# Three exponentials ahead of each pair of silus, a held GpSimd product, and a new set of places, in a fused Mamba and SwiGLU layer

## The chip, the cores and the metric

The kernel runs on one core of a Trainium2 chip. A core has five engines that run their own instruction lists and meet only at semaphores: TensorE (PE, matrix products and transposes into PSUM), VectorE (DVE), ScalarE (ACT, functions by table), GpSimd (POOL, which works on SBUF alone) and SyncE (SP, which issues transfers). The metric is the time of one launch on the device, in microseconds.

## The reference, cut to what matters

One layer over 4 sequences of 2048 rows of 256 values (8192 rows), all in float32:

```python
x_and_res = x @ W_in                                  # 256 -> 512 + 512
x_in, res = split(x_and_res)
x_conv = silu(causal_depthwise_conv4(x_in))           # "u" below
dt, B, C = split(x_conv @ W_x)                        # 16, 16, 16 columns
delta = softplus(dt @ W_dt + b_dt)
h = exp(delta * A) * h + delta * B * x_conv           # per row, 16 states for each of 512 channels
y = sum over states of C * h, plus x_conv * D
x = layernorm(x + (y * silu(res)) @ W_out)
gate, up = x @ wg.T, x @ wu.T                         # 256 -> 768, integer weights / 127
x = layernorm(x + (silu(gate) * up) @ wd.T)
```

The recurrence over the rows is the part that can't be made a matrix product. The 512 channels are 4 blocks of 128 partitions, so there are 64 recurrences (16 states by 4 blocks) for each stretch of rows.

## The kernel before, in words

The rows are cut into 16 chunks of 512 columns (time runs along the free axis). A chunk has 64 **beats**; beat b is state b // 4 and channel block b % 4. In each beat

- ACT computes `da = exp(delta * a)` (`exp`, L1086), into one of two PSUM banks in turn;
- POOL computes the product `dbu = du * B` (`times_b`, L1228) into one of DBU = 4 buffers of SBUF; the product of beat b waits until the scan of beat b - 4 has ended;
- DVE runs the scan `h = da * h + dbu` (`scan`, L1423);
- PE transposes h in 128 x 128 blocks (`turns`, L729), so that the sum over the 16 states can be taken with C as a per-partition scalar: half of the rows by ACT (`weigh`, L1095) and PE's accumulation (L754), the other half by DVE (`sum_states`, L1435, after each odd beat, 30 times in a chunk).

Everything else is fitted around the beats, with half a beat as the unit. While chunk i is scanned, the front of chunk i + 1 (the projection `xin` and `res`, the convolution `conv`, `dtb`, `ct`, `dt`) and the back of chunk i - 1 (turning the sums `yt`, the output projection `o`, the layer norm, turning its result `x1t`, `gate`, `up`, `down`, the second layer norm) are worked off. Their order is a table written by a planner: FILL_AT says in which beat PE issues each matmul group ("fill"), BANK in which of two PSUM banks it lands, READ_AT in which half beat ACT or DVE reads it, BEAT when the other steps of ACT and POOL come. A place of 64 and more means a beat of the next chunk, a negative one a beat of the chunk before. Nothing is dynamic: each engine's list has a fixed order, and an engine that waits holds up everything behind it. EARLY_FILL and EARLY_READ are the places of chunk 1's `xin` and `conv`, which are made during chunk 0. POOL has, beside its product in each beat, a tiny copy of the last column of h (`carry`, L1286) in each fourth beat, twelve more full-size products in a chunk (`times z` 4, L1279; `add u` 4, L1260; `times u` 4, L1267) and eight normalisations of 128 x 256 (L1252).

ACT holds one set of functions at a time. Exponential and logarithm are in one set, silu in another. So the silus of a chunk are gathered in two places ("windows"), each with a pair of them: `silu uz` (u of the next chunk and z, at 31 and 32) and `silu gate` (the two halves of the gates, at 43 and 45). At the start of a window ACT computes the exponentials of the next AHEAD = 2 beats at once, into buffers of SBUF called `da_ahead` (`between`, L1142), then loads the silu set (L1159), does the first silu, what lies between, the second one, loads the exponential set again (L1171), and computes the exponential of the beat after. The scans of these two beats (32 and 33, 44 and 45) read `da_ahead`, all other scans read a PSUM bank. Both kinds have the same line, L1423. The buffers are told apart in the trace by their names.

The normalisations of POOL lie at 27 (four, first layer norm) and at 96, 103, 108, 108 (second one, that is in beats 32, 39, 44, 44 of the chunk after). `times z` lies at 12, 12, 15, 17; `add u` at 52, 55, 62, 62 and `times u` at 53, 59, 63, 63.

## Time and profile before

| | |
|---|---|
| median of 3 runs | 1836.55 us (1835.42 to 1837.67) |
| profiled execution, its own time | 1836.67 us |
| its span | 1834.9 us |
| what lies around the span | 1.8 us |
| busy: DVE, PE, POOL, ACT | 1718.8, 1691.5, 1654.9, 1605.0 us |
| granted clock of TensorE, mean | 0.993 |

Busy is the time in which an engine had an instruction under way, waits for semaphores left out. All four are between 87% and 94% of the span, so no one of these shares names a bound. A scan, a product and an exponential are 128 x 512 float32 each. In the rows below the first number of a timeline line is the start in us from the span's start, the second the length; lines of the same kind that follow each other without a pause are put together, with their number behind the x; in brackets stands the idle time ahead of it and what ended that.

### The profile page before, as it was taken

To read this page: it belongs to the slowest core of one execution; us is meant where nothing else is said; L and a number is where in the kernel's file an instruction comes from. 1 tells how busy PE (TensorE), PEld (TensorE's weight loads), DVE (VectorE), ACT (ScalarE), POOL (GpSimd) and SP (SyncE) were. 2 spreads that over 40 slices of the span, in tenths; PEclk is the share of its full clock that TensorE was granted. 3 is DMA by queue.
4 is the path that set the end of the run, shared out by engine and by line. 5 is a ranking of instruction groups with operands and counts; after the bars stand their busy time and mean duration, and the time that the engine had idled before them with its cause. 6 is when DMAs were issued, how large, how long until landed. Compare 5 with 4: busy or idle time off the path is not lost.

```text
span 1834.9 us, 32556 instructions
## 1 busy us (share of the span) xinstructions
PE 1691.5 (92%) x10128; PEld 1270.3 (69%) x10128; DVE 1718.8 (94%) x1958; ACT 1605.0 (87%) x2769; POOL 1654.9 (90%) x1629
## 2 busy tenths in 40 slices
PE   8878898998989999898998989999898999988788
PEld 3546676776767677676776767677676776767667
DVE  4899999999999999999999999999999999999994
ACT  4797989989898998989889898998989899898874
POOL 2899899998999989999998999989899998999970
PEclk9999999999999999999999999999999999999999
DMA  7212213232222322313222322323222222211110
GB/s 239 104 59 104 82 59 121 73 119 71 104 92 70 115 71 104 105 66 119 78 108 72 113 82 73 113 70 115 94 82 104 82 104 81 105 70 58 35 47 24
DMA packets 82108, 164.57 MB, mean 90 GB/s; under 512 B 10369, under 2 KB 28033, under 8 KB 81938
## 3 DMA queue, kind: packets, MB, share of 16 engines
q1 hardware_dynamic: 80498, 160.90, 25.2%
q8 instruction: 85, 1.39, 0.3%
q10 hardware_dynamic: 1440, 1.58, 0.3%
q14 instruction: 85, 0.70, 0.1%
HBM read 87.47 MB, written 8.91 MB: 53 GB/s over the span
## 4 chain that ended last, share of the span: by engine, by line
PE 60%; ACT 16%; POOL 8%; issue 8%; DVE 6%; DMA 1%; DVEq 0%; SPq 0%; ACTq 0%; POOLq 0%
PE ht_upper L729 8%; PE ht_lower L729 8%; PE fill L665 8%; PE y_upper L754 8%; PE fill L551 7%; POOL dbu L1228 6%; PE fill L634 6%; DVE h L1423 5%; PE fill L655 3%; ACT da L1086 3%; PE fill L604 3%; PE fill L566 3%; ACT gt L1095 2%; ACT z L980 2%; PE fill L626 1%
## 5 line engine op out<-in xcount | busy, mean ns | idle before, releaser
L1228 POOL TENSOR_TENSOR dbu<-du,brep 128x512 f32<-128x512 f32 x1024 | 1315.2, 1315 | 115.0 <-DVE h L1423 88.5
L1423 DVE TENSOR_TENSOR_SCAN h<-da,carry,dbu 128x512 f32<-128x512 f32 x960 | 1184.5, 1268 | 41.7 <-ACT da L1086 37.1
L1086 ACT ACTIVATE da<-delta,a_s 128x512 f32<-128x512 f32 x960 | 654.8, 692 | 79.2 <-DVE h L1423 72.3
L1095 ACT ACTIVATE gt<-ht_upper,ct 128x512 f32<-128x512 f32 x512 | 350.1, 684 | 69.3 <-PE ht_upper L729 66.0
L729 PE MATMUL ht_upper<-ident,h 128*128 128x128 f32 x2048 | 314.8, 276 | 71.6 <-ACT gt L1095 51.0
L729 PEld LDWEIGHTS ht_upper<-ident,h 128*128 128x128 f32 x2048 | 242.6, 142 | 195.3 <-issue 130.7
L1435 DVE SCALAR_TENSOR_TENSOR acc<-ht_lower,ct,acc 128x512 f32<-128x512 f32 x480 | 349.2, 727 | 8.2 <-PE ht_lower L729 6.8
L729 PE MATMUL ht_lower<-ident,h 128*128 128x128 f32 x2048 | 312.3, 275 | 27.0 <-DVE acc L1435 23.0
L754 PE MATMUL y_upper<-ident,gt 128*128 128x128 f32 x2048 | 309.6, 274 | 0.9 <-ACT kb L912 0.9
L729 PEld LDWEIGHTS ht_lower<-ident,h 128*128 128x128 f32 x2048 | 239.2, 142 | 80.8 <-DVE h L1423 39.4
L754 PEld LDWEIGHTS y_upper<-ident,gt 128*128 128x128 f32 x2048 | 246.2, 141 | 51.1 <-issue 37.4
L551 PE MATMUL fill<-xt_s,win_s 128*128 128x512 f32 x456 | 223.3, 597 | 11.7 <-DVE x1t L1356 11.7
L665 PE MATMUL fill<-wd_s,kb 128*128 128x256 f32 x720 | 177.7, 380 | 0.0
L665 PEld LDWEIGHTS fill<-wd_s,kb 128*128 128x128 f32 x720 | 127.4, 190 | 18.3 <-issue 6.7
L634 PE MATMUL fill<-wout_s,kb 128*128 128x256 f32 x480 | 122.4, 383 | 0.7 <-DVE xr L1334 0.7
L1423 DVE TENSOR_TENSOR_SCAN h<-da_ahead,carry,dbu 128x512 f32<-128x512 f32 x64 | 118.6, 1874 | 0.0
L551 PEld LDWEIGHTS fill<-xt_s,win_s 128*128 128x128 f32 x456 | 74.5, 190 | 55.1 <-issue 55.1
L655 PE MATMUL fill<-x1t,wu_s 128*128 128x512 f32 x360 | 109.1, 431 | 0.4 <-DVE kb L1345 0.4
L655 PE MATMUL fill<-x1t,wg_s 128*128 128x512 f32 x360 | 106.5, 417 | 0.0
L634 PEld LDWEIGHTS fill<-wout_s,kb 128*128 128x128 f32 x480 | 85.3, 190 | 21.3 <-issue 12.8
L655 PEld LDWEIGHTS fill<-x1t,wu_s 128*128 128x128 f32 x360 | 64.2, 189 | 23.3 <-issue 6.7
L1260 POOL TENSOR_TENSOR delta<-delta,du 128x512 f32<-128x512 f32 x60 | 76.3, 1288 | 0.8 <-issue 0.3
(189 smaller groups left out, 1883.0 us busy)
## 6 DMA issues: line engine op xcount, KB each, us to landing
brep<-b_rows SPq DMA_DIRECT2D x127, 512.0 KB, 3.7
xs<-xin SPq DMA_DIRECT2D x242, 256.0 KB, 2.5
xr<-x SPq DMA_DIRECT2D x16, 512.0 KB, 5.5
xt_s<-x_t SPq DMA_DIRECT2D x15, 512.0 KB, 3.7
...
```

Of the source, the lines that this page charges most:

```text
L551: mm = nc.tensor.matmul(front_bank(c, name)[:, :], win_s[:, k, m * P:(m + 1) * P], xt_place(c)[:, k, :], start=(k == 0), stop=(k == KK - 1))
L634: mm = nc.tensor.matmul(fill_bank(name)[:, 0:DM], kb[:, m, t * P:(t + 1) * P], wout_s[:, m, :], start=(m == 0), stop=(m == DB - 1))
L655: mm = nc.tensor.matmul(fill_bank(name)[:, :], w[:, k, n * P:(n + 1) * P], x1t[:, half, k, :], start=(k == 0 and half == 0), stop=(k == KK ...
L665: mm = nc.tensor.matmul(fill_bank(name)[:, 0:DM], kb[:, n, t * P:(t + 1) * P], wd_s[:, n, :], start=(n == 0), stop=(n == HB - 1))
L729: mm = nc.tensor.transpose(bank[:, m * P:(m + 1) * P], h[:, n % 2, m, t * P:(t + 1) * P], ident[:, :])
L754: mm = nc.tensor.matmul(y_upper[m // 2][:, (m % 2) * HALF + k * P:(m % 2) * HALF + (k + 1) * P], lhsT=gt[:, (n * UPPER + k) % GT, m * P:(m ...
L1086: nc.scalar.activation(dst[:, :], delta[:, par, m, :], ACT.Exp, scale=a_s[:, m, n:n + 1])\
L1095: nc.scalar.activation(gt[:, (n * UPPER + k) % GT, :], ht_upper[:, :], ACT.Copy, scale=ct[:, par, k, n:n + 1])\
L1228: nc.gpsimd.tensor_tensor(dbu[:, beat % DBU, :], du[:, par, m, :], brep[:, n // PIECE % 2, n % PIECE, :], ALU.mult).then_inc(dbu_ready, 1)
L1260: nc.gpsimd.tensor_tensor(delta[:, par, m, :], delta[:, par, m, :], du[:, par, m, :], ALU.add)\
L1423: nc.vector.tensor_tensor_scan(h[:, n % 2, m, 0:T], da[beat % 2][:, :] if slot is None else da_ahead[:, slot, :], dbu[:, beat % DBU, :], c ...
L1435: nc.vector.scalar_tensor_tensor(out=acc[:, par, k, :], in0=ht_lower[:, :], scalar=ct[:, par, UPPER + k, n:n + 1], in1=acc[:, par, k, :], ...
```

## The change

- AHEAD is 3: the three exponentials of beats 31, 32, 33 and of beats 43, 44, 45 are made ahead, and three scans in each window read SBUF. `da_ahead` grows by a buffer. To make room, four small constants are put into one tensor.
- HOLD = (4, 5): the product of beat 35 (start of the first window, 30, + 1 + 4) waits until the scan of beat 33 has ended instead of that of beat 31, and the product of beat 48 (42 + 1 + 5) until that of beat 45 instead of 44.
- The windows move: `silu uz` to 30.5 and 32, `silu gate` to 42 and 43.5.
- All places are new: most fills, reads and norms lie half a beat to four beats earlier. `times z` lies at 7, 9, 13, 15, `add u` at 51, 55, 60, 63, `times u` at 52, 56, 63, 63, the first normalisations at 25, the second ones at 94, 100, 104, 112 (beats 30, 36, 40, 48).
- The early places of chunk 1's `xin` and `conv` are spread over beats 1 to 26 of chunk 0 instead of 0 to 16. Because of the new order, PE's first fill in each bank now waits for what chunk 0's front left there (`wait_first`).

```diff
-FILL_AT = {"xin1": (0, 1), "xin2": (1, 2), "xin3": (5, 5), "yt0": (7,), "yt1": (9,), "conv0": (9,),
...
+FILL_AT = {"xin2": (1, 1), "xin3": (3, 5), "yt0": (6,), "yt1": (7,), "conv0": (8,), "o0": (9, 9, 9, 10),
+           "o1": (11, 11, 11, 11), "conv1": (12,), "o2": (13, 14, 15, 15), "o3": (15, 16, 16, 16), "conv2": (18,),
+           "res0": (19, 21), "res1": (22, 24), "conv3": (22,), "x1t0": (24,), "x1t1": (25,), "res2": (29, 30),
+           "gate0": (31, 31), "res3": (32, 33), "gate1": (35, 35), "gate2": (37, 37), "gate3": (37, 37),
+           "gate4": (38, 38), "gate5": (38, 39), "dtb": (40, 40, 40, 41), "up0": (43, 43), "up1": (43, 43),
+           "up2": (44, 44), "ct": (45,), "dt0": (45,), "up3": (47, 47), "up4": (47, 48), "dt1": (48,), "dt2": (50,),
+           "up5": (50, 50), "down0": (51, 51, 51, 51, 53, 53), "dt3": (51,), "down1": (53, 55, 56, 56, 56, 56),
+           "xin0": (-10, -9), "down2": (56, 59, 59, 59, 59, 59), "down3": (60, 60, 60, 62, 63, 63), "xin1": (-1, -1)}
...
-EARLY_FILL = {"xin0": (0, 0), "xin1": (1, 1), "xin2": (2, 2), "xin3": (3, 3), "conv0": (5,), "conv1": (8,),
-              "conv2": (11,), "conv3": (14,)}
-EARLY_READ = {"xin0": 1, "xin1": 2, "xin2": 3, "xin3": 4, "conv0": 7, "conv1": 10, "conv2": 13, "conv3": 16}
+EARLY_FILL = {"xin0": (1, 1), "xin1": (3, 3), "xin2": (3, 4), "xin3": (6, 7), "conv0": (4,), "conv1": (12,),
+              "conv2": (18,), "conv3": (26,)}
+EARLY_READ = {"xin0": 1, "xin1": 5, "xin2": 5.5, "xin3": 8.5, "conv0": 9.5, "conv1": 13.5, "conv2": 22.5, "conv3": 26}
...
-BEAT = {"soft exp": [49, 51, 57, 59.5], "soft ln": [49, 52.5, 59.5, 59.5], "add u": [52, 55, 62, 62],
-        "times u": [53, 59, 63, 63], "x1 cut": [30, 35], "x1 low": [29.5, 30.5], "y upper": [5.5, 6],
-        "times z": [12, 12, 15, 17], "mean": [20.5, 73.5], "rstd": [25.5, 83], "shift": [27, 83],
-        "square": [(21, 21, 21, 23), (79.5, 79.5, 82, 82)], "norm": [(27, 27, 27, 27), (96, 103, 108, 108)],
-        "halo": -17.5, "silu uz": [31, 32], "silu gate": [43, 45]}
+BEAT = {"soft exp": [47.5, 51, 55, 57.5], "soft ln": [48.5, 52, 56, 59], "add u": [51, 55, 60, 63],
+        "times u": [52, 56, 63, 63], "x1 cut": [27, 29.5], "x1 low": [28, 28], "y upper": [5.5, 6.5],
+        "times z": [7, 9, 13, 15], "mean": [19, 67], "rstd": [23, 82], "shift": [25, 90],
+        "square": [(19.5, 19.5, 19.5, 20.5), (67, 75, 75, 76.5)], "norm": [(25, 25, 25, 25), (94, 100, 104, 112)],
+        "halo": -25.5, "silu uz": [30.5, 32], "silu gate": [42, 43.5]}
...
-AHEAD = 2
+AHEAD = 3
+DBU = 4
+HOLD = (4, 5)
...
+HELD = {start + 1 + HOLD[n]: start + AHEAD for n, start in enumerate(SILUS) if HOLD[n]}
+assert all(last < product < 64 and product - last <= DBU for product, last in HELD.items())
...
-        ones_row = sb("ones_row", [XD, 1])
-        convb_s = sb("convb_s", [P, DB])
-        d_s = sb("d_s", [P, DB])
-        eps_s = sb("eps_s", [P, 1])
+        consts = sb("consts", [P, 2 * DB + 2])
+        convb_s, d_s = consts[:, 0:DB], consts[:, DB:2 * DB]
+        ones_row, eps_s = consts[:, 2 * DB:2 * DB + 1], consts[:, 2 * DB + 1:2 * DB + 2]
...
+                elif (c, name) in held_before:
+                    wait_first([n for n in FIRST_FILLS if front_bank(0, n) is front_bank(c, name)][-1])
...
-                after(pool, h_ready, i * NH + beat + 1 - DBU)
+                used = beat - DBU if beat >= DBU else max(b for b in range(NH) if b % DBU == beat) - NH
+                after(pool, h_ready, i * NH + max(used, HELD.get(beat, used)) + 1)
```

READ_AT and BANK are new in the same way; of READ_AT the places that matter below are up0 and up1 at 44 (before 44.5 and 45), res2 at 32 (31.5), dtb at 43 (45).

## Rows read from the trace of the kernel before

**Rows 1.** Windows (length; busy: PE, PEld, DVE, ACT, POOL; PEclk, DMA): chunks 0, 1-14, 15, 4.
```profile
33.75:149.96 116.21, 88.23 (x479) 56.30 (x479) 101.36 (x98) 91.91 (x146) 102.83 (x97) 0.94 0.26 93
149.96:1685.43 1535.47, 1451.16 (x8784) 1096.96 (x8783) 1483.06 (x1653) 1395.84 (x2409) 1451.57 (x1424) 1.00 0.26 91
1685.43:1791.29 105.86, 85.07 (x535) 70.20 (x533) 103.81 (x114) 83.66 (x139) 93.52 (x93) 0.95 0.12 41
...
478.05:587.50 109.45, 103.80 (x631) 78.47 (x630) 106.13 (x121) 99.83 (x173) 103.83 (x103) 1.00 0.27 93
```

**Rows 2.** Groups by line: busy us, mean ns, idle before them, releasers.
```profile
L1228 POOL TENSOR_TENSOR dbu<-du,brep 128x512 f32<-128x512 f32 x1024 | 1315.2, 1315 | 115.0 <-DVE h L1423 88.5 <-DVE brep L1504 19.7 <-DVE du L1498 3.1
L1423 DVE TENSOR_TENSOR_SCAN h<-da,carry,dbu 128x512 f32<-128x512 f32 x960 | 1184.5, 1268 | 41.7 <-ACT da L1086 37.1 <-issue 2.6 <-POOL dbu L1228 1.8
...
L1423 DVE TENSOR_TENSOR_SCAN h<-da_ahead,carry,dbu 128x512 f32<-128x512 f32 x64 | 118.6, 1874 | 0.0
```

**Rows 3.** POOL's waits in chunk 4: total us, times, longest.
```profile
POOL dbu L1228 <- DVE h L1423: 4.7, 7, 1.8
POOL stats L1247 <- ACT stats L1006: 0.5, 1, 0.5
```

**Rows 4.** Timeline of DVE, first window of chunk 3 (beats 31 to 35).
```profile
418.81 0.72 DVE L1435 SCALAR_TENSOR_TENSOR acc<-ht_lower,ct,acc 128x512 f32<-128x512 f32 x1
419.45 4.08 DVE L1423 TENSOR_TENSOR_SCAN h<-da_ahead,carry,dbu 128x512 f32<-128x512 f32 x2
...
424.90 2.47 DVE L1423 TENSOR_TENSOR_SCAN h<-da,carry,dbu 128x512 f32<-128x512 f32 x2 [0.72 <-ACT da L1086]
```

**Rows 5.** Timeline of POOL, same window (products of beats 33 to 39).
```profile
417.52 3.76 POOL L1228 TENSOR_TENSOR dbu<-du,brep 128x512 f32<-128x512 f32 x3
421.19 1.15 POOL L1286 COPY carry<-h 128x4 f32<-128x4 f32 x1
422.44 3.39 POOL L1228 TENSOR_TENSOR dbu<-du,brep 128x512 f32<-128x512 f32 x2
426.26 2.53 POOL L1228 TENSOR_TENSOR dbu<-du,brep 128x512 f32<-128x512 f32 x2 [0.43 <-DVE h L1423]
428.73 0.19 POOL L1286 COPY carry<-h 128x4 f32<-128x4 f32 x1
```

**Rows 6.** Timeline of DVE, chunk 3's second window (from beat 44).
```profile
440.33 1.27 DVE L1423 TENSOR_TENSOR_SCAN h<-da_ahead,carry,dbu 128x512 f32<-128x512 f32 x1
442.24 0.69 DVE L1345 SCALAR_TENSOR_TENSOR kb<-fill,kb 128x512 f32<-128x512 f32 x1 [0.64 <-PE fill L655]
442.85 2.28 DVE L1423 TENSOR_TENSOR_SCAN h<-da_ahead,carry,dbu 128x512 f32<-128x512 f32 x1
```

**Rows 7.** Timeline of POOL, same window (products 45 to 47, 49 to 51).
```profile
437.98 4.69 POOL L1228 TENSOR_TENSOR dbu<-du,brep 128x512 f32<-128x512 f32 x3
...
445.21 1.27 POOL L1228 TENSOR_TENSOR dbu<-du,brep 128x512 f32<-128x512 f32 x1 [1.16 <-DVE h L1423]
448.24 2.54 POOL L1228 TENSOR_TENSOR dbu<-du,brep 128x512 f32<-128x512 f32 x2 [1.76 <-DVE h L1423]
```

**Rows 8.** Timeline, start of chunk 3: POOL's first products, DVE's first scans.
```profile
367.13 5.02 POOL L1228 TENSOR_TENSOR dbu<-du,brep 128x512 f32<-128x512 f32 x4
368.63 2.46 DVE L1423 TENSOR_TENSOR_SCAN h<-da,carry,dbu 128x512 f32<-128x512 f32 x2
```

**Rows 9.** Timeline of ACT, first window of chunk 3.
```profile
415.44 1.33 ACT L1086 ACTIVATE da_ahead<-delta,a_s 128x512 f32<-128x512 f32 x2
...
424.17 0.69 ACT L1086 ACTIVATE da<-delta,a_s 128x512 f32<-128x512 f32 x1
```

**Rows 10.** Timeline, chunk 0: PE's second `xin`, ACT's read of it.
```profile
37.81 6.45 PE L551 MATMUL fill<-kb,win_s 128*128 128x512 f32 x8 [3.87 <-ACT xin L912]
41.60 0.60 ACT L912 ACTIVATE xin<-fill 128x512 f32<-128x512 f32 x1 [3.35 <-PE fill L551]
```

**Rows 11.** Windows: chunk 0, beats 2 and 3.
```profile
38.00:42.00 4.00, 4.00 (x5) 1.61 (x6) 2.00 (x3) 0.65 (x2) 3.09 (x3) 0.50 0.68 262
```

More of the change, by code:

```diff
@@ L23 @@
 SILU_SET = "silu_and_others"
-FILL_AT = {"xin1": (0, 1), "xin2": (1, 2), "xin3": (5, 5), "yt0": (7,), "yt1": (9,), "conv0": (9,),
[8 rows of a table removed]
+FILL_AT = {"xin2": (1, 1), "xin3": (3, 5), "yt0": (6,), "yt1": (7,), "conv0": (8,), "o0": (9, 9, 9, 10),
[7 rows of a table added]
 FILLS = list(FILL_AT)
 FRONT = ("xin", "conv", "res", "dtb", "ct", "dt")
-BANK = {"xin1": 0, "xin2": 1, "xin3": 1, "yt0": 0, "yt1": 1, "conv0": 0, "o0": 0, "conv1": 1, "o1": 0, "o2": 1,
[4 rows of a table removed]
+BANK = {"xin2": 0, "xin3": 0, "yt0": 1, "yt1": 0, "conv0": 1, "o0": 0, "o1": 1, "conv1": 0, "o2": 1, "o3": 0,
[4 rows of a table added]
 F_FILLS = sorted((name for name in FILLS if name.rstrip("0123456789") in FRONT), key=lambda name: FILL_AT[name][-1])
@@ L57 @@
 GT = 4
-READ_AT = {"xin0": -2.5, "conv0": 11, "res0": 23.5, "xin1": 2.5, "conv1": 16, "res1": 27, "xin2": 4.5, "conv2": 25.5,
[5 rows of a table removed]
-BEAT = {"soft exp": [49, 51, 57, 59.5], "soft ln": [49, 52.5, 59.5, 59.5], "add u": [52, 55, 62, 62],
-        "times u": [53, 59, 63, 63], "x1 cut": [30, 35], "x1 low": [29.5, 30.5], "y upper": [5.5, 6],
-        "times z": [12, 12, 15, 17], "mean": [20.5, 73.5], "rstd": [25.5, 83], "shift": [27, 83],
-        "square": [(21, 21, 21, 23), (79.5, 79.5, 82, 82)], "norm": [(27, 27, 27, 27), (96, 103, 108, 108)],
-        "halo": -17.5, "silu uz": [31, 32], "silu gate": [43, 45]}
+READ_AT = {"xin0": -6.5, "conv0": 10.5, "res0": 22, "xin1": 2, "conv1": 15.5, "res1": 26, "xin2": 3, "conv2": 21,
[5 rows of a table added]
+BEAT = {"soft exp": [47.5, 51, 55, 57.5], "soft ln": [48.5, 52, 56, 59], "add u": [51, 55, 60, 63],
[3 more added lines that the diff above has]
+        "halo": -25.5, "silu uz": [30.5, 32], "silu gate": [42, 43.5]}
 FIRST_FILLS = ["xin0", "xin1", "xin2", "xin3", "conv2", "conv0", "conv1", "conv3", "dtb", "dt0", "dt1", "ct", "dt2", "dt3"]
@@ L171, in mamba_swiglu @@
     GROUPS = P // GROUP
-    DBU = 4
     x_flat = x.rearrange("r d -> (r d)")
@@ L536, in wait_bank, with wait_first @@
             def wait_bank(c, name):
-                if (c, name) in held_before:
-                    if held_before[c, name]:
-                        pe.wait_ge(*taken(*held_before[c, name]))
+                if (c, name) in held_before and held_before[c, name]:
+                    pe.wait_ge(*taken(*held_before[c, name]))
+                elif (c, name) in held_before:
+                    wait_first([n for n in FIRST_FILLS if front_bank(0, n) is front_bank(c, name)][-1])
                 elif FIRST_AT[name] >= FIRST_BANKS:
-                    held = FIRST_FILLS[FIRST_AT[name] - FIRST_BANKS]
-                    signal, count = taken(0, held)
-                    pe.wait_ge(signal, FIRST_CONVS.index(int(held[-1])) + 1 if held[:4] == "conv" else count)
+                    wait_first(FIRST_FILLS[FIRST_AT[name] - FIRST_BANKS])
+            def wait_first(held):
+                signal, count = taken(0, held)
+                pe.wait_ge(signal, FIRST_CONVS.index(int(held[-1])) + 1 if held[:4] == "conv" else count)
             def in_proj(c, name, m, k):
```

24 rows, old and new, of tables (BANK, FILL_AT, READ_AT) are left out of this document.

## The prediction

> **What bounds the kernel now.** The busy shares come first: DVE, PE and POOL are all busy for over 90% of the span, so the bound must be read from one chunk. The windows view shows it [rows 1]: a steady chunk lasts 109.45 us, DVE works 106.13 of it, PE 103.80, POOL 103.83, ACT 99.83. Nobody has more than 10 us to spare, and two engines are separated by 2 us.
>
> Next, the groups by line [rows 2]. Scans that read `da` from PSUM last 1.27 us, those that read `da_ahead` from SBUF 1.87 on average. The work is the same; something stops them. The two timelines of a window, side by side, say what. Scan 32 is issued at 419.45 while POOL is in product 34, and the scans of beats 32 and 33 together end at 423.53 [rows 4]. POOL's three products 33, 34, 35 run without a break to 421.28, each at its usual length [rows 5]. So scan 32 stood still until product 35 was through, although that one, 1.27 long, was begun only at 420.0. Then the sides change: the tiny carry copy takes 1.15 instead of 0.19, and the pair of products 36 and 37 3.39 instead of 2.53 [rows 5]. While one engine has a float32 operation with two operands in SBUF under way the other one stands still, and products that follow each other without a pause keep a waiting scan out. Scans with `da` in PSUM beside the same products last 1.27 us: they are free of it.
>
> The third look is at who has slack. POOL waits for scans (its four buffers full) for 4.7 us in chunk 4 and for the layer norm 0.5 [rows 3], and rows 7 show where: 1.16 and 1.76 after beats 45 and 47. At the start of a chunk there is none: four products end at 372.15, the first began at 367.13, so product 0 ended at 368.40 to 368.45, and scan 0 began at 368.63 [rows 8]. The lead that POOL has at beat 50 is used up by the products for the next chunk (`add u`, `times u`), and it then runs with no reserve until the windows. I therefore take POOL as the engine that sets the period as soon as a few tenths of its slack in the windows are taken.
>
> **Removed: ACT's late exponential.** From the first exponential ahead at 415.44 to the end of exponential 34 at 424.86 ACT needs 9.4 us [rows 9], and scan 34 waits 0.72 for it [rows 4]; over the run DVE waits 37.1 us for `da` [rows 2]. A third exponential ahead lets that chain start a scan earlier. Worth by itself: the 0.72, at most 1.0 us a chunk. But the time that the lock takes lies in the same window and hides the same ACT chain: scans 32 and 33 took 4.08 instead of the 2.45 of two free ones, 1.63 lost, and then the wait came to 0.72. One without the other gives nothing.
>
> **Added: two scans per chunk that lock POOL, and the holds.** POOL's own work in a chunk: 103.83 busy, less what was standing still: 1.15 - 0.19 = 0.96 and 3.39 - 2.53 = 0.86 [rows 5], and 4.69 against 3.76 for three products = 0.93 [rows 7, 5]. That leaves 101.1 us, and the change removes none of it. The period is 101.1 plus the time in which POOL may not or can't work. Before, this was 109.45 - 101.1 = 8.4.
>
> After, first window. POOL comes into it with no lead: scan 31 is issued about when product 33 is in progress, and 33 and 34 run through, as 34 and 35 did. Product 35 is held, so POOL stands from the end of product 34 to the end of scan 33. Two such scans ended 423.53 - 421.28 = 2.25 after the product [rows 4, 5]; a third is 2.47 - 1.27 = 1.20 more, and the sum between scans 31 and 32 is 419.45 - 418.81 = 0.64 [rows 4]. With 0.1 for the signal: 4.2 us. Second window: products 45 and 46 run through while scan 43 waits; then scan 43 alone, 1.05 + 0.1; product 47; then it is held during scan 44, two `up` products of 442.85 - 442.24 = 0.61 [rows 6], and scan 45: 2.25 + 1.2 + 0.1 = 3.55. Together 4.7. Nothing else should stop POOL: after both holds it is behind, so its buffers are not full, and the 0.5 for the layer norm goes, since rstd and shift now lie eight beats apart. New period: 101.1 + 4.2 + 4.7 = 110.0. What is queued behind the held products: only POOL's own list (norms at 36 and 48, the next products); scan 35 waits for the first, and at 1.24 us after scan 33 it is there while scan 34 runs, so DVE sees little of it. It sees the loss at scan 31 (about 2 us) and at scans 43 and 44 (2.1 and 0.6), together more than the 1.63 and the 2.28 - 1.27 = 1.01 [rows 6] before.
>
> Fourteen chunks took 1535.47, 109.68 each [rows 1]: +0.35 x 14 = **+5 us**. Bounds: if scan 31 slips in ahead of product 34, which then runs during the sum, the first window costs POOL 3.4 instead of 4.2, the period is 109.2, -7 us; if it is issued during product 32 (as if POOL were a product further behind) DVE loses 1.2 more with every chunk in which it has no reserve, +1.1 each, +16 us.
>
> A rule speaks to this. The Trainium skill ("SBUF — State Buffer", Who interferes with whom) calls the shared ports an exclusive lock held for the whole instruction, and has issue order decide who blocks. By that order scan 31 would go ahead of product 34, and the sum would be the -7 us of the lower bound. The trace agrees with the lock and not with the order: scan 32 was issued at 419.45, some 0.5 ahead of product 35, and was served after it.
>
> **Moved: places.** `times z` at 7 and 9 instead of 12 and 12, norms at 25 instead of 27: the same POOL work earlier, so DVE meets POOL at beat 10 instead of beat 13. For POOL's chain that is nothing; DVE's short waits for it replace its waits for ACT there. `dtb` is two beats earlier and `up0`, `up1` wait for PE no longer (0.64 in rows 6), but scan 45 is behind a hold either way: 0 to -0.5 a chunk, taken 0, hidden by POOL's chain. The SyncE queue keeps its order; conv1's shifted copies have four beats as before, others more: 0. The constants in one tensor: 0. The wait of PE for the bank in chunk 0: its holder has long been read, 0.
>
> **Chunk 0** is the one place where spreading pays. ACT reads `xin1` in beat 2 and stands 3.35 us for it [rows 10], because PE sat idle 3.87 before and then ran at 0.50 of its clock, the lower level [rows 11]; exponential 3, and so scan 3, is behind that read. In all DVE is idle for 116.21 - 101.36 = 14.8 us of chunk 0 [rows 1]. With reads at 5, 5.5 and 8.5 scan 3 doesn't wait, 3.3 us; the two reads behind it, which I take at half of that each (their fills lie behind the same slow one), give 3.3 more; some 2.5 come back at beats 5 and 6, where ACT then has both reads and the first weighings, each as long as an exponential. That is 4 by beat 8, and I take 2 more for the spread `conv` reads by beat 20. The two windows of chunk 0 cost 2 more than now, as above. **-4 us** (0 to -7, half of what is idle).
>
> **Chunk 15** (105.86 [rows 1]) has no products for a next chunk, so DVE sets its end. From product 34's end to scan 45's end it takes after the change 4.2 for the hold, 12 products at 1.24 (three in 3.76 [rows 5]), 3 copies and 2 norms of half a product's size (16.4), 1.1 for scan 43, 1.3 for product 47 and 3.4 to the end of scan 45, 26.4 in all; before, in chunk 3, from 421.28 - 1.24 to 442.85 + 2.28 it was 25.1 [rows 5, 6], and it is less where no u is to be made. **+3 us** (1 to 4).
>
> **Sum.** +5 - 4 + 3 = +4. The profiled execution took 1836.67 (span 1834.9 and 1.8 around it, which stays), 0.1 over the median: 1840.6, rounded to **1840.5**. From no change this is at the edge of what can be told, 0.2% or 3.7 us.
>
> **Rivals.** (1) Faster, the windows fit: scan 31 arrives just as a product ends and gets in, as scan 44 did at 440.33, which lasted 1.27 [rows 6]. Period 109.4 (between the 109.2 of the bound and 109.6), chunk 0 gains 6, the last loses 1: 1836.6 + 14 x (-0.3) - 6 + 1 = 1827. For it: DVE gets rid of ACT's wait and comes earlier, so where it meets a product's end isn't fixed. Against it: POOL has no reserve when it enters, and every lock that it meets costs its own time. Chance 0.30. (2) Nothing: chunk 0's gain and the windows' loss cancel, period 109.8: 1836.6 + 2 - 4 + 2 = 1837. Chance 0.18. (3) Slower, and clearly: scan 31 is issued while product 32 is in progress and waits for three; place: beats 30 and 31, where POOL has a norm before product 31; price 1.2 us a chunk on DVE and 0.7 on the period, from the point where POOL's lead at beat 31 is under a third of a product. Period 110.8: 1836.6 + 15.7 - 3 + 3 = 1852. Chance 0.20. (4) The hold does nothing, as POOL reaches product 35 only after scan 33: period as before, 1833 with chunk 0's gain; part of (1). The forecast keeps 0.32.
>
> **Chances.** The forecast lies half within 0.2% (up to 1840.2) and half above. Slower: 0.20 + 0.16 + a tenth of (2) and other surprises 0.05 = 0.41. Same: 0.16 + 0.12 = 0.28. Faster: 0.31. The range takes in both rivals and a little more on either side: 1824 to 1856; the likeliest case alone is 1837 to 1845.
>
> **What would show it.** Right: scans on `da_ahead` 96, in each chunk scan 31 about 3.3 long with products 33 and 34 beside it, scans 32 and 33 at 1.27; POOL's wait ahead of product 35 about 4 us and ahead of 48 about 3.5, and next to no other POOL waits; DVE waits for `dbu` appear in beats 0 to 16; the wait for `da` at 34 is gone; steady chunks 110.0. Wrong: POOL still has waits of over 2 us a chunk for full buffers outside the holds (then DVE or PE sets the period), scan 31 under 2.5, chunks under 109.3; or chunk 0 not shorter than 113.

## The result and the profile after

| | before | after |
|---|---|---|
| median of 4 runs on the same chip | 1836.12 us | 1824.66 us (1823.48 to 1827.21) |
| profiled execution: time, span | 1836.67, 1834.9 us | 1827.21, 1825.4 us |
| chunk 0 | 116.21 | 110.21 us |
| chunks 1 to 14, each | 109.68 | 109.26 us |
| chunk 15 | 105.86 | 108.95 us |

The ratio after to before is 0.9938 (95% interval 0.9925 to 0.9951): 0.6% faster, where the forecast was 0.2% slower. It lies inside the range, on the other side of "same". The spans differ by 9.5 us: 6.0 in chunk 0, 5.8 in chunks 1 to 14, 0.8 after the last scan (its cause was not looked for), and 3.1 the other way in chunk 15. The forecast had -4, +5, 0 and +3 for these. So one term is to be explained, the steady chunk.

The windows view of the kernel after (chunks 0, 1 to 14, 15; columns as in [rows 1]):

```profile
33.86:144.07 110.21, 86.77 (x483) 55.81 (x482) 100.99 (x98) 92.20 (x146) 101.54 (x97) 0.95 0.29 99
144.07:1673.73 1529.66, 1443.93 (x8783) 1099.26 (x8782) 1473.80 (x1652) 1390.75 (x2409) 1447.50 (x1424) 1.00 0.26 91
1673.73:1782.68 108.95, 87.41 (x535) 71.94 (x533) 106.79 (x116) 83.08 (x138) 90.68 (x93) 0.94 0.11 40
```

The groups by line, beside [rows 2]: 96 scans read `da_ahead`, and their mean fell from 1.87 to 1.55 us, for most of them are not stopped. The wait for `da` went up, not away (37.1 to 42.5).

```profile
L1236 POOL TENSOR_TENSOR dbu<-du,brep 128x512 f32<-128x512 f32 x1024 | 1315.1, 1314 | 120.6 <-DVE h L1431 97.0 <-DVE brep L1512 19.8 <-DVE du L1506 3.1
L1431 DVE TENSOR_TENSOR_SCAN h<-da,carry,dbu 128x512 f32<-128x512 f32 x928 | 1151.6, 1271 | 54.7 <-ACT da L1093 42.5 <-issue 6.5 <-PE ht_lower L736 3.6
L1431 DVE TENSOR_TENSOR_SCAN h<-da_ahead,carry,dbu 128x512 f32<-128x512 f32 x96 | 147.2, 1547 | 0.0
```

**Where in a chunk.** Cut a chunk at the starts of scans 0, 16, 25, 31, 35, 42 and 46: the stretches between tell more than any mean over the chunk. First chunk 3 before, then chunk 3 after:

```profile
368.63:392.98 24.35, 24.27 (x156) 17.82 (x154) 23.52 (x27) 22.01 (x40) 24.35 (x24) 1.00 0.25 90
...
407.23:417.62 10.39, 8.64 (x62) 5.93 (x60) 10.32 (x13) 10.34 (x19) 10.29 (x15) 1.00 0.35 126
417.62:426.10 8.48, 5.66 (x25) 3.20 (x26) 7.76 (x8) 8.44 (x10) 8.11 (x6) 1.00 0.24 68
426.10:437.32 11.22, 11.15 (x74) 9.45 (x73) 10.95 (x12) 11.08 (x20) 10.07 (x11) 1.00 0.18 67
437.32:446.89 9.57, 8.76 (x38) 5.34 (x38) 8.93 (x10) 9.51 (x13) 8.00 (x8) 1.00 0.35 100
446.89:478.05 31.16, 31.04 (x192) 25.62 (x191) 30.41 (x38) 26.42 (x46) 29.29 (x28) 1.00 0.26 86
```

```profile
362.93:388.08 25.15, 25.15 (x165) 19.28 (x164) 24.04 (x27) 22.18 (x44) 25.15 (x25) 1.00 0.27 97
...
402.40:412.62 10.22, 7.87 (x52) 5.70 (x51) 10.22 (x12) 10.19 (x18) 10.22 (x12) 1.00 0.14 46
412.62:420.50 7.88, 5.11 (x30) 3.29 (x29) 6.44 (x8) 7.85 (x9) 5.51 (x7) 1.00 0.14 33
420.50:431.65 11.15, 11.15 (x67) 8.87 (x66) 10.97 (x13) 11.14 (x21) 11.14 (x12) 1.00 0.23 78
431.65:441.04 9.39, 8.68 (x49) 6.18 (x48) 8.99 (x11) 9.00 (x12) 6.35 (x5) 1.00 0.21 62
441.04:472.10 31.06, 31.06 (x184) 25.28 (x183) 30.53 (x40) 26.15 (x45) 31.06 (x31) 1.00 0.30 102
```

Beats 31 to 35 took 8.48 and take 7.88 (-0.60), and in both ACT has work for all but 0.04 of it, POOL for 8.11 and for 5.51. Beats 25 to 31 gain 0.17, 35 to 46 0.25, 46 to 64 0.10. The first 16 beats give back 0.80, the nine behind them 0.07. Net: 109.42 to 109.17.

### The profile page after: what moved, and what is told of

The parts are those of the page before. It is cut to its first block and busy times, and to the rows that moved or that the text cites. A ratio compares the mean times of both kernels' runs of the same rounds, so it can differ in the third digit from the quotient of the medians.

```text
span 1825.4 us, 32557 instructions
## 1 busy us (share of the span) xinstructions
PE 1683.4 (92%) x10128; PEld 1272.4 (70%) x10128; DVE 1711.8 (94%) x1958; ACT 1599.6 (88%) x2769; POOL 1646.8 (90%) x1629
## 5 line engine op out<-in xcount | busy, mean ns | idle before, releaser
L1431 DVE TENSOR_TENSOR_SCAN h<-da,carry,dbu 128x512 f32<-128x512 f32 x928 | 1151.6, 1271 | 54.7 <-ACT da L1093 42.5
L1093 ACT ACTIVATE da<-delta,a_s 128x512 f32<-128x512 f32 x928 | 641.6, 700 | 38.7 <-DVE h L1431 36.0
L736 PEld LDWEIGHTS ht_upper<-ident,h 128*128 128x128 f32 x2048 | 247.9, 141 | 215.8 <-issue 127.9
L558 PE MATMUL fill<-xt_s,win_s 128*128 128x512 f32 x456 | 230.2, 598 | 18.3 <-DVE x1t L1364 18.3
L1431 DVE TENSOR_TENSOR_SCAN h<-da_ahead,carry,dbu 128x512 f32<-128x512 f32 x96 | 147.2, 1547 | 0.0
L1287 POOL TENSOR_TENSOR kb<-kb,z 128x512 f32<-128x512 f32 x60 | 77.8, 1297 | 0.0
```

The costliest lines, as they stand in the source:

```text
L558: mm = nc.tensor.matmul(front_bank(c, name)[:, :], win_s[:, k, m * P:(m + 1) * P], xt_place(c)[:, k, :], start=(k == 0), stop=(k == KK - 1))
L736: mm = nc.tensor.transpose(bank[:, m * P:(m + 1) * P], h[:, n % 2, m, t * P:(t + 1) * P], ident[:, :])
L1093: nc.scalar.activation(dst[:, :], delta[:, par, m, :], ACT.Exp, scale=a_s[:, m, n:n + 1])\
L1287: nc.gpsimd.tensor_tensor(kb[:, blocks, times], kb[:, blocks, times], z[:, par, blocks, times], ALU.mult)\
L1431: nc.vector.tensor_tensor_scan(h[:, n % 2, m, 0:T], da[beat % 2][:, :] if slot is None else da_ahead[:, slot, :], dbu[:, beat % DBU, :], c ...
```

## What the windows look like now

DVE in the first window of chunk 3 (beats 31 to 35), beside [rows 4]:

```profile
412.62 1.26 DVE L1431 TENSOR_TENSOR_SCAN h<-da_ahead,carry,dbu 128x512 f32<-128x512 f32 x1
413.80 0.73 DVE L1443 SCALAR_TENSOR_TENSOR acc<-ht_lower,ct,acc 128x512 f32<-128x512 f32 x1
414.44 2.77 DVE L1431 TENSOR_TENSOR_SCAN h<-da_ahead,carry,dbu 128x512 f32<-128x512 f32 x2
417.13 0.72 DVE L1443 SCALAR_TENSOR_TENSOR acc<-ht_lower,ct,acc 128x512 f32<-128x512 f32 x1
419.30 2.47 DVE L1431 TENSOR_TENSOR_SCAN h<-da,carry,dbu 128x512 f32<-128x512 f32 x2 [1.44 <-ACT da L1093]
```

POOL beside it (products 32 to 34, 35), to compare with [rows 5], and in the second window (46 and 47, 48), with [rows 7]:

```profile
410.25 4.70 POOL L1236 TENSOR_TENSOR dbu<-du,brep 128x512 f32<-128x512 f32 x3
417.29 1.26 POOL L1236 TENSOR_TENSOR dbu<-du,brep 128x512 f32<-128x512 f32 x1 [2.34 <-DVE h L1431]
...
433.00 3.42 POOL L1236 TENSOR_TENSOR dbu<-du,brep 128x512 f32<-128x512 f32 x2 [0.50 <-DVE h L1431]
436.37 1.11 POOL L1294 COPY carry<-h 128x4 f32<-128x4 f32 x1
440.02 1.27 POOL L1236 TENSOR_TENSOR dbu<-du,brep 128x512 f32<-128x512 f32 x1 [2.54 <-DVE h L1431]
```

Scan 31 is 1.26 long, not 3.3. Three products that should take 3.76 took 4.70: product 33 ends near 412.76, scan 31 was issued 0.14 before that and got in, and product 34 stood instead. Scans 32 and 33 lose 0.3 together. Exponential 34 then ends the window; its chain in ACT's timeline, beside [rows 9]:

```profile
409.22 1.95 ACT L1093 ACTIVATE da_ahead<-delta,a_s 128x512 f32<-128x512 f32 x3
411.19 1.28 ACT L1166 ACT_TABLE_LOAD   x1
412.49 1.92 ACT L983 ACTIVATE u<-u 128x2048 f32<-128x2048 f32 x1
414.31 0.66 ACT L1102 ACTIVATE gt<-ht_upper,ct 128x512 f32<-128x512 f32 x1
414.88 0.58 ACT L919 ACTIVATE z<-fill 128x512 f32<-128x512 f32 x1
415.35 1.91 ACT L987 ACTIVATE z<-z 128x2048 f32<-128x2048 f32 x1
417.28 1.28 ACT L1178 ACT_TABLE_LOAD   x1
418.57 0.69 ACT L1093 ACTIVATE da<-delta,a_s 128x512 f32<-128x512 f32 x1
```

No waits stand in brackets: ACT goes from 409.22 to 419.26 without a pause, and scan 34 starts 0.04 after its end.

In the second window scan 43 is free. Scan 44 is issued at 435.16, 0.02 after product 47 has begun, and stands until that product has ended (2.34, 1.07 lost), beside [rows 6]:

```profile
432.84 1.26 DVE L1431 TENSOR_TENSOR_SCAN h<-da_ahead,carry,dbu 128x512 f32<-128x512 f32 x1
434.50 0.75 DVE L1443 SCALAR_TENSOR_TENSOR acc<-ht_lower,ct,acc 128x512 f32<-128x512 f32 x1 [0.40 <-PE ht_lower L736]
435.16 2.34 DVE L1431 TENSOR_TENSOR_SCAN h<-da_ahead,carry,dbu 128x512 f32<-128x512 f32 x1
```

One thing is new at the start of a chunk. In the kernel before, scan 0 waited for no product; now it waits 0.38 us. The profile names no releaser, but the scan begins 0.09 after product 0 has ended:

```profile
362.93 2.52 DVE L1431 TENSOR_TENSOR_SCAN h<-da,carry,dbu 128x512 f32<-128x512 f32 x2 [0.38 <-issue]
```

POOL has no gap from the start of product 48 (440.02) to scan 16 of the next chunk, which again begins 0.09 after its product (chunks 3 and 4). So what the forecast said of POOL, that it has no reserve there, is what the kernel after shows.

## The experiments

Ratios are to the kernel before in runs on the same chip; "chunk" is the usual length of a steady one. "The lock" is what [rows 4, 5] show: a scan that reads `da` from SBUF and a POOL product keep each other standing. The theories: P, POOL sets the period (the forecast's); H and others as each text names them; and the one that is left at the end, **W**: DVE, idle for 3.5% of a chunk, sets it outside the windows, ACT's uninterrupted work sets the first window, and the lock adds to the second.

**1. The holds** (e1, e2, e3; each the kernel after, with this line changed)

```diff
-HOLD = (4, 5)
+HOLD = (0, 0)      # e2: (4, 0), e3: (0, 5)
```

> The changed kernel with HOLD = (0, 0): products 35 and 48 wait as before the change, for scans 31 and 44. Theory P (POOL sets the period of the changed kernel: its own 101.1 us of work a chunk plus the time in which it is locked out or held): product 35 then runs while scan 32 waits, about 1.2 us, and scan 32 lasts some 3 us; DVE loses nothing by it, as scan 34 waits 1.44 us for its exponential anyway. POOL stands 0.4 us less in the first window and 1.2 less in the second, and the wait of scan 0 for its product (0.36) goes: 109.17 becomes 108.8 to 109.0, 3 to 5 us faster than the changed kernel, so 1820 to 1822. Theory H (the holds keep the scans free, and that is where the gain comes from): 1.2 us a chunk are lost again, 109.17 becomes 110.2, about 1840.

> The changed kernel with the first hold alone, HOLD = (4, 0). Theory P: product 48 runs beside the two up products and ends about when scan 45 is issued (scan 45 loses 0.2 at most), POOL is 1.2 us ahead after it, the wait of scan 0 goes (0.36): 0.2 to 0.4 us a chunk, 1819 to 1822. Theory H: the second hold saves scan 45 the 1.0 us that it lost before the change: 109.17 becomes 110.2, 1840.

> The changed kernel with the second hold alone, HOLD = (0, 5). Theory P: as the run without holds for the first window: scan 32 lasts about 3 us, the wait of scan 34 for its exponential (1.44) shrinks by what scan 32 loses, POOL gains 0.4: no more than 0.4 us a chunk, 1819 to 1825. Theory H: 1.2 us a chunk lost, 1842.

Measured: 1823.54 us, 0.9919 [0.9904, 0.9935]; 1825.73, 0.9931 [0.9917, 0.9945]; 1823.98, 0.9927 [0.9911, 0.9944]. The after kernel's interval overlaps all three: the holds are worth nothing in the time that can be told. The chunk is 109.13, 109.13, 109.19, against 109.17. Without holds scan 33 is stopped for 0.96, and the wait for exponential 34 falls from 1.44 to 0.48: the first window is 7.88 with and without its hold. The second hold does move something: with it beats 46 to 64 take 31.06 instead of 30.74 (POOL has 1.10 us of idle time there without it, none with it), and beats 42 to 46 (9.39 for 9.53) and 0 to 16 (25.15 for 25.32) give 0.31 of it back. Nor does POOL stand less without the holds: its busy time in chunks 1 to 14 is 1488.50 us instead of 1447.50, as it now stands inside its products, stopped by the lock. Chunk 15 moves too, 107.3 without holds.

**2. Two exponentials ahead in the new table** (e4)

```diff
-AHEAD = 3
+AHEAD = 2
```

> The changed kernel with AHEAD = 2, all places as changed; products 35 and 48 are held for scans 32 and 44. If the third exponential ahead is what the windows gained by: scan 33 waits for the exponential made after both silus, until about 6 us after scan 31's end where 2.5 were free, so scans 33 and 34 together come 1.2 us a chunk later than now, scan 45 about 0.6 later: 1.2 to 1.8 us a chunk, 1842 to 1851. If the gain is all in the places and POOL: two locks of POOL fewer a chunk, 2 us less standing, but DVE bound: 1824 or a little less.

Measured: 1854.41 us, 1.0081 [1.0064, 1.0098]. Beats 31 to 35 take 9.10. Scan 33 waits for its exponential, which is now behind both silus (DVE, first window of chunk 3):

```profile
419.70 1.59 DVE L1431 TENSOR_TENSOR_SCAN h<-da_ahead,carry,dbu 128x512 f32<-128x512 f32 x1
423.95 1.28 DVE L1431 TENSOR_TENSOR_SCAN h<-da,carry,dbu 128x512 f32<-128x512 f32 x1 [2.65 <-ACT da L1093]
```

**3. The early places, alone and left out** (e5: the kernel before with the new EARLY_FILL, EARLY_READ and `wait_first`; e6: the kernel after with the old EARLY_FILL and EARLY_READ)

> The kernel before with the new EARLY_FILL and EARLY_READ alone (and the wait of PE for the bank in chunk 0). Both traces put the first chunk at 116.2 and 110.2 us. If the early places alone do that: chunk 0 becomes 110 to 111, everything else stays, 5 to 6 us faster than the kernel before, 1830.5. If the main table's new places for chunk 0 (res reads at 22 to 35, norms) or the third exponential did part of it: 2 to 4 us.

> The changed kernel with the old EARLY_FILL and EARLY_READ. If the early places are worth the 6.0 us of chunk 0: 1824.7 + 6 = 1830.7, chunk 0 at 116. If only half: 1827.5.

Measured: e5 1835.11 us, 0.9995 [0.9985, 1.0006], chunk 0 112.96; e6 1835.66, 1.0002 [0.9993, 1.0011], chunk 0 124.81, the rest as in the kernel after (109.12). The two chunk lengths are from single executions, and these were the fastest of e5's eleven (1831.17) and the slowest of e6's (1839.77), so either may overstate. In the old table the early places show 3 us of chunk 0's span there, and nothing that the median of 11 runs can tell; in the new one they are worth some 11 us of the time (14.6 in the profiled chunk 0). In e6 DVE waits 5.1 us in beat 15 for PE, which the old table does not have. The forecast's -4 for chunk 0 was a sum over one table; the -6 measured is what a new table with matching early places gives.

**4. The third exponential in the old table** (e8: AHEAD = 3 and the code for it in the kernel before, all places old, no holds; e7: the same with HOLD = (4, 5))

> The changed kernel with all tables of places of the kernel before (silus at 31, 32 and 43, 45), three exponentials ahead and the holds (now products 36 and 49, held for scans 34 and 46). Theory P: POOL's reserve was 0.15 us a chunk and its standing grows by two scans and the hold gaps, from 8.4 to about 8.9: 109.45 becomes 109.9, and 110 with a collision at scan 32: 1843 to 1850. Rival (three ahead pays by itself, DVE sets the period): the wait of scan 34 moves to scan 35 and shrinks from 0.72 by 1: 0.7 to 1 us a chunk faster, 1821 to 1826.

> The same without holds. Theory P: scans 32, 33 and 34 read SBUF, the first or second of them waits for the products that are free to run (up to 2.5 us), POOL's standing stays near 8.4: within 3 us of the kernel before, 1833 to 1840. Rival: the holds are what makes three ahead pay, then this one is slower by 1 us a chunk, 1850.

Measured: e8 1844.46 us, 1.0048 [1.0035, 1.006], chunk 109.82; e7 1855.74, 1.0106 [1.0091, 1.0122], chunk 110.65. The windows of e8 in chunk 3, beats 31 to 35 and 35 to 42:

```profile
422.12:430.07 7.95, 5.17 (x20) 2.68 (x20) 7.95 (x7) 7.91 (x8) 7.85 (x6) 1.00 0.14 38
430.07:442.11 12.04, 11.31 (x75) 9.82 (x76) 11.20 (x13) 11.55 (x21) 11.14 (x12) 1.00 0.26 83
```

The third exponential gains 0.53 in the window, with the lock as it was, and the old places lose 0.82 right behind it, where a `sum_states` waits 0.51 for PE's `ht_lower`, and exponential 36 comes 0.20 late. In the new table that stretch is 11.15. The two holds together cost 0.83 a chunk here and nothing there.

**5. ACT's chain in the first window** (e9, e10: after with and without holds; e11: without holds, exponential 34 behind the weighing of beat 33)

```diff
-                nc.scalar.activation(z[:, par, :, :], z[:, par, :, :], ACT.Silu).then_inc(z_ready, 1)
+                nc.scalar.activation(z[:, par, 0:DB // 2, :], z[:, par, 0:DB // 2, :], ACT.Silu).then_inc(z_ready, 1)
```

> The changed kernel, but the silu of z covers two of the four channel blocks, so ACT's work between its two table loads is about 0.85 us shorter in the first window; nothing else changes (the output is computed with half of z without its silu). Theory L (the period is a loop: PE has no idle time outside the windows and inside them waits for ACT's chain of exponentials, loads and silus): the chain is 0.85 shorter, PE and DVE gain that, until POOL binds; with the holds POOL has only the 0.5 us that it waits before product 46: 0.5 to 0.85 us a chunk, 14 chunks, 1813 to 1818. Theory P (POOL's work and its standing in the windows alone set the period): the hold of product 35 lasts until scan 33, which is before ACT's late part, so 0: 1824.

> The same without holds. Theory L: POOL has 2 us of idle time in beats 41 to 47, so all of the 0.85 comes through: 1823.5 - 12 = 1811.5, and 2 to 5 us faster than the one with holds. Theory P: 1823.5.

> The changed kernel without holds, with exponential 34 moved behind the weighing of beat 33 (which PE waits for, 1.67 us in its last wait of the window). Theory L in its narrow form (PE's wait for the weighing is the loop): PE goes on 0.6 us sooner, scan 34 starts 0.6 later, which DVE has to make up by beat 43: up to 0.5 us a chunk faster, 1817 to 1823. If scan 34 itself is in the loop: 0.6 us a chunk slower, 1832.

Measured: e9 1821.22 us, 0.9917 [0.990, 0.993], chunk 108.94; e10 1812.78, 0.9874 [0.986, 0.9889], chunk 108.46; e11 1829.3, 0.996 [0.9948, 0.9973], chunk 109.59. In e10 ACT has 9.9 / 14 = 0.71 us less to do in a chunk than in e1 (1391.07 and 1381.20 busy in chunks 1 to 14), and the chunk is 0.67 shorter; e11 puts one operation of 0.67 into the chain, and the chunk is 0.46 longer. Beats 31 to 35 of e10 take 0.54 less. ACT is still busy all the time, but the wait for exponential 34 (0.48 in e1) is gone and DVE has no gap either:

```profile
412.52:419.86 7.34, 5.42 (x32) 3.59 (x31) 7.34 (x7) 7.31 (x9) 7.34 (x7) 1.00 0.11 20
```

With holds (e9) beats 31 to 35 gain even 0.84, but scan 43 is then issued 0.50 before the end of product 45, product 46 goes ahead of it too, and it stands for 1.55: most is given back in the second window (9.98 for 9.39).

**6. The lock** (e12: after, no holds, all scans read PSUM; e16: the kernel before with the same)

```diff
...
-                nc.vector.tensor_tensor_scan(h[:, n % 2, m, 0:T], da[beat % 2][:, :] if slot is None
-                                             else da_ahead[:, slot, :], dbu[:, beat % DBU, :],
+                nc.vector.tensor_tensor_scan(h[:, n % 2, m, 0:T], da[beat % 2][:, :], dbu[:, beat % DBU, :],
...
```

> The changed kernel without holds in which every scan reads a PSUM bank: the exponentials of the windows are still computed ahead into SBUF, but the six scans read what an earlier beat left in their bank (wrong values, same work). So no scan locks POOL or waits for it. What the lock costs: scans 32, 33, 44, 45 last 1.27 (they lose 0.32 + 0.96 + 1.07 + 0.14 now). Theory L: the first window's 1.3 us only lengthens scan 34's wait for its exponential (0.48 to 1.8), the second one's 1.2 counts as far as PE and ACT let it: 0.3 to 1.0 us a chunk, 1810 to 1819. Theory P: POOL stands 3.5 us less a chunk, the period falls to DVE's own, 107: 1793.

> The kernel before, in which scans 32, 33, 44 and 45 read a PSUM bank instead of da_ahead (the exponentials ahead are still computed, their results are not used, so h is not the reference's in these beats); the four scans are free of the lock. 'One without the other gives nothing' (first window: the 1.63 of lock hides ACT's chain to exponential 34): the wait of scan 34 grows from 0.7 to about 2.3 and only the second window's 1.0 is gained: 14 x 1.0 = 14 us, 1820 to 1825. Rival: the lock costs its full 2.6 a chunk: 1796 to 1802. Rival: POOL binds before too, and gains 0.96 + 0.86 + 0.93 of standing still where DVE's lead allows: also 1796 to 1805, but with POOL's waits unchanged.

Measured: e12 1807.53 us, 0.9843 [0.9829, 0.9856], chunk 108.26 (0.87 less than e1); e16 1827.72, 0.9951 [0.9934, 0.9967], chunk 108.8. In e16 the first window of chunk 3 reads:

```profile
418.54 2.45 DVE L1420 TENSOR_TENSOR_SCAN h<-da,carry,dbu 128x512 f32<-128x512 f32 x2
420.91 0.75 DVE L1431 SCALAR_TENSOR_TENSOR acc<-ht_lower,ct,acc 128x512 f32<-128x512 f32 x1
423.99 2.47 DVE L1420 TENSOR_TENSOR_SCAN h<-da,carry,dbu 128x512 f32<-128x512 f32 x2 [2.33 <-ACT da L1084]
```

and the windows view gives for beats 31 to 35 and 42 to 46

```profile
416.70:425.19 8.49, 5.66 (x25) 3.20 (x26) 6.16 (x8) 8.45 (x10) 6.27 (x6) 1.00 0.25 69
...
436.40:445.32 8.92, 8.79 (x39) 5.38 (x38) 8.04 (x11) 8.86 (x11) 7.09 (x8) 1.00 0.25 72
```

The two scans are free, DVE has 1.6 us less to do, and the window is as long as with the lock (8.49, 8.48), as the wait behind it grows by the same amount. In the second window the lock is not hidden: 9.57 becomes 8.92, and with three exponentials ahead 9.53 (e1) becomes 8.67. The first window is 7.88 in e1 and in e12.

**7. POOL's work** (e13: before, e14: after, e15: after without holds; the first layer norm on a quarter of its columns)

```diff
-                nc.gpsimd.tensor_scalar(xr[:, par, t, :], xr[:, par, t, :], rstd[:, which, t:t + 1],
+                cols = DM if which else DM // 4
+                nc.gpsimd.tensor_scalar(xr[:, par, t, 0:cols], xr[:, par, t, 0:cols], rstd[:, which, t:t + 1],
```

> The kernel before, with the first layer norm (four at beat 27) normalising only a quarter of its columns: 4 x 0.56 us of POOL's work become about 4 x 0.18, so POOL has 1.5 us less to do in each chunk, ahead of the first window. The layer norm's result is therefore not the reference's in the other columns. The theory of the forecast (P: POOL sets the period): 15 chunks x 1.5 us less, limited by DVE's own waits, 1814 to 1820. The loop (L: PE's fills, ACT's exponentials and silus in the windows and the scans behind them set it; POOL's 4.7 us of waits for full buffers are real reserve): 1834 to 1837, POOL's waits grow by the 1.5. Mixed (POOL co-binds, as in the kernel after): 1826 to 1832.

> The same cut (first layer norm on a quarter of its columns, 1.5 us of POOL's work less in each chunk, ahead of the first window) in the kernel after, with its holds. POOL alone binds: 1802 to 1808. The loop alone binds: 1823 to 1826. Co-binding, POOL by some tenths in a chunk: 1817 to 1822. More lead for POOL also moves the point at which scan 31 meets a product; if it meets product 34 in its middle, its lock costs 1 us and takes back what was gained.

> The same cut in the kernel after without holds (HOLD = (0, 0)), which took 1823.5. There POOL had more reserve than with the holds, so the loop says 1821 to 1824 (no change), POOL alone 1803 to 1810.

Measured: 1837.73 us, 1.0001 [0.9989, 1.0012]; 1824.94, 0.9933 [0.9917, 0.995]; 1822.42, 0.992 [0.9905, 0.9936]. The cut was less than I had counted on: the group's mean fell from 562 to 480 ns over both sizes, so a quarter of the columns takes 0.40, and POOL is relieved of 4 x 0.16 = 0.65 us a chunk, 10 us over the run. Of these 10 us nothing comes out in the steady chunks (109.45, 109.17, 109.14; the interval of e13 ends at 2 us of gain); chunk 15 of the profiled executions is 1.1 us shorter in e14 and 2.2 in e15, and 0.8 longer in e13. POOL's waits in chunk 3 of e13, beside [rows 3] (chunk 3 of the kernel before has the same 4.7), show where they went:

```profile
POOL dbu L1228 <- DVE h L1424: 5.4, 7, 1.8
```

What this tests is narrow: the work went at beats 25 and 27, behind the beats in which POOL has no lead (0 to 16) and right ahead of the windows, in which it stands anyway.

**8. PE's work** (e17: before, e18: after; `down` on half of its columns, beats 51 to 63)

```diff
-                mm = nc.tensor.matmul(fill_bank(name)[:, 0:DM], kb[:, n, t * P:(t + 1) * P], wd_s[:, n, :],
+                mm = nc.tensor.matmul(fill_bank(name)[:, 0:DM // 2], kb[:, n, t * P:(t + 1) * P], wd_s[:, n, 0:DM // 2],
```

> The kernel before, in which the last projection (down, 24 matmuls of a chunk in beats 51 to 63) computes half of its columns; the other half of the second layer norm's input is what was left in the bank. PE has between 2 and 5 us less to do in each chunk, far from both windows. The PE loop (PE's queue full from one window to the next): the period falls by at least 1 us, limited by DVE's own work: 1810 to 1822, and PE gets idle time in beats 51 to 63. DVE's bound (its own work plus what it loses in the windows to the lock and to ACT): only the 0.46 wait for a down fill at beat 63.5 can go, 14 x 0.3 = 4 us at most: 1832 to 1837.

> The same cut (down on half of its columns) in the kernel after. The PE loop: the period falls by 0.5 us or more until POOL, which has the holds, takes over: 1808 to 1818. DVE's bound, or POOL's: 1822 to 1826, no change, as DVE nowhere waits for a down fill there.

Measured: 1835.55 us, 0.9994 [0.9984, 1.0003]; 1823.24, 0.9933 [0.9919, 0.9948]. PE is busy for 35 us less in chunks 1 to 14 of e17 and 44 less in those of e18, and neither kernel is faster. A loop of PE's queue from window to window, which the first twelve runs had made me believe in, falls with this. In the kernel after PE has no gap in beats 0 to 16 (25.15) and 46 to 64 (31.06); in e18 it has 1.11 and 1.99 us of them, and the two stretches are as long as before:

```profile
362.34:387.47 25.13, 24.02 (x154) 18.04 (x153) 24.04 (x27) 22.05 (x44) 25.13 (x25) 1.00 0.27 97
...
440.43:471.49 31.06, 29.07 (x194) 23.17 (x193) 30.49 (x40) 26.60 (x46) 31.06 (x31) 1.00 0.29 102
```

So an engine without a gap in a stretch need not be what bounds it.

**What is left** is W, and its two windows are shown: e10 and e11 (ACT's chain in the first, 0.67 for 0.71), e16 and e12 (the lock costs nothing in the first window and 0.65 to 0.86 in the second). That POOL alone does not set the period is shown by e10 and e11: they leave its work and its places alone, theory P gave no change for e10, and the chunk moves by -0.67 and +0.46 us. "DVE outside the windows" is argued: DVE is idle for 2.0 of 91.9 us there, e17 and e18 exclude PE in the last beats and make it unlikely in the first 16, and no run took work from DVE alone. A rival stands untested: POOL in beats 46 to 16 of the kernel after, where it has no gap and scan 0 waits for it. In e1, where POOL has 1.10 us of idle time in beats 46 to 64 and scan 0 waits 0.04, these beats together take 56.06 instead of 56.21; a run that takes work from POOL at these places would settle the rest.

## Why the prediction was wrong, step by step

- **"I therefore take POOL as the engine that sets the period": the step that failed.** The reading behind it was a lead of next to nothing at beats 0 to 1, which is so, and the sum "101.1 plus the time in which POOL may not or can't work". That sum is an identity. It holds for every engine of every kernel, and it holds after the change too: 2.34 for the hold and 4.70 - 3.76 for product 34 are 3.3, in the second window 0.50 + 0.89 + 0.92 + 2.54 are 4.85, and 101.1 + 8.1 is 109.2. So within the sum the term that was off is the first window's standing time, 4.2 forecast and 3.3 measured. The sum becomes a forecast only if the standing time is known ahead and no other term gives way, and in e13 a term gave way at once (4.7 to 5.4). The runs show what stands in its place. In the first window it is ACT's chain: 0.71 us less of it, with POOL's work as it was, makes the chunk 0.67 shorter (e10). In the second it is what the lock costs DVE, 0.65 to 0.86 (e16, e12). [Rows 3] had said part of it: 4.7 us of waits for full buffers are reserve. The reading that POOL has none ahead of the windows was right (scan 0 waits 0.38 for it), but it does not set the length of the chunk as a whole.
- **"POOL comes into it with no lead: scan 31 is issued about when product 33 is in progress": wrong by about half a product.** It was issued in the last 0.14 of product 33 and got in. That is rival (1) in its mechanism, and its time, 1827, is 2 us off. Of the signs named in advance for a wrong forecast two came, scan 31 under 2.5 and chunks under 109.3; POOL's waits outside the holds, 0.50 us in chunk 3, did not. In chunk 0 scan 31 was 3.3 long and in chunk 15 2.7, as forecast for all.
- **The order rule.** In the steady chunks scan 31 went ahead of product 34, which stood behind it, and this gives the 109.2 that I had worked out for that case. The Trainium skill ("SBUF — State Buffer", Who interferes with whom) has issue order decide; here the trace agrees. In chunk 15 it does not: scan 31 was issued at 1723.00, 0.29 ahead of product 34, and was served after it, as scan 32 in [rows 4]. What differs is how long before the end of the running product the scan came: 0.14 in the steady chunks and 0.17 for scan 44 in [rows 6], which got in, and 0.36 in chunk 15, 0.50 in e9 and 0.60 for [rows 4], which did not. Too late is possible as well: scan 43 of chunk 15, issued 0.08 before the end of product 44, was kept out by two products and lasted 3.65. Behind a product that had itself been standing 0.50 was enough: in e1 scan 32, issued at 414.73, went ahead of product 35 as product 34 ended at 415.23. So issue order alone does not tell who goes first, and a forecast should carry both cases.
- **The second window: total right, parts wrong.** Forecast 4.7 us of standing for POOL, measured 4.9. But scan 43, from which 2.1 was to be lost, is free, and scan 44 loses 1.07, not 0.6.
- **The holds: the forecast had them cost, and they cost nothing in a steady chunk** (e1 to e3), because what the first one spares DVE in the first window is time that ACT's chain covers, and what the second one costs in beats 46 to 64, 0.32, is given back in the second window (0.14) and in beats 0 to 16 (0.17).
- **The third exponential, "0.72, at most 1.0": near. "One without the other gives nothing": right in one direction only.** Taking the lock away alone gave nothing in the first window (e16, 8.49 against 8.48). The third exponential alone, with the lock as it was, gave 0.53 there (e8), and in the new table it is worth 1.22 (9.10 in e4, 7.88 in the kernel after). And the wait for `da` at scan 34, which was to be gone, is twice as long, 1.44 for 0.72, as scans 31 to 33 lose 0.3 us to the lock where scan 32 lost 1.6.
- **The moved places, taken at 0: wrong, by 0.7 us a chunk for the better (three ahead, no holds) and up to 2 for the worse (two ahead).** (old places, two ahead) 109.45, (old, three) 109.82, (new, two, holds) 110.7 to 111.6, (new, three) 109.17. Neither part pays alone. In the new table scan 31 and exponential 34 come earlier against the fills, and beats 35 to 42, which cost e8 0.82, cost nothing.
- **Beats 0 to 16, not in the forecast: +0.80.** Of this 0.37 are waits (0.30 at beat 7 for PE's `ht_lower`, 0.48 for 0.41 at beat 8), and 0.42 is one more read of an `o` fill by DVE, which lay behind beat 16 before; at beat 31 the chunk is still 0.70 behind. POOL too has one operation more in this stretch (25 for 24, `times z` at 15) and no gap in either kernel; which of these sets the 25.15 no run tells apart. So the moved places cost something here before they pay in the window.
- **Chunk 0, -4: -6.0.** The waits at beats 3 to 5 (2.78, 1.42, 1.45) fell to one of 0.25, and 2.53 and 0.90 came back at beats 6 and 8, as the forecast said some would. TensorE's granted clock was 0.57 in these beats, next to the lower level, after PE had idled 3.00 us; it had been 0.50 [rows 11]:

```profile
38.00:42.00 4.00, 3.29 (x6) 0.98 (x6) 3.71 (x5) 1.95 (x4) 2.98 (x3) 0.57 0.71 262
```

- **Chunk 15, +3: +3.1, by the mechanism forecast.** From the end of product 34 to the end of scan 45 it takes 26.47, where the sum had 26.4, and it took 22.63 in chunk 15 of the kernel before. Without the lock the whole chunk is 103.6 (e12), without the holds 107.3 (e1). The forecast's long scan 31 and long hold are both there:

```profile
1720.83 3.77 POOL L1236 TENSOR_TENSOR dbu<-du,brep 128x512 f32<-128x512 f32 x3
1728.77 1.27 POOL L1236 TENSOR_TENSOR dbu<-du,brep 128x512 f32<-128x512 f32 x1 [4.17 <-DVE h L1431]
```

- **"The SyncE queue keeps its order ...: 0": off by 1.5 us in all.** In chunks 5 and 12 of the kernel before PE waits 1.61 and 1.37 us for the shifted copies of `conv3`, and these two chunks take 111.0; after, with `xin3` read at 6.5 and the fill at 22 instead of 9 and 26, the waits are 0.58 and 0.63, in chunks of 110.06 and 109.89. PE's timeline before, chunk 5:

```profile
629.97 1.06 PE L566 MATMUL fill<-xs,taps 128*32 128x512 f32 x8 [1.61 <-DMA xs<-xin]
```

What I should have read is what the mean of 109.68 beside a usual chunk of 109.45 was asking for. The sum set the 110.0 of a usual chunk against that mean; against the usual chunk the same terms give 0.55 x 14 = +7.7, not +5.

No kernel of the series that computes all of the reference is faster than the kernel after by more than the measurement tells; e1, without holds, is the simplest of equals.
